# A decoder layer with a state-space mixer: the first pass in another order, and the parameters' copy one step earlier

## What is computed

```python
proj = layernorm(x) @ in_proj_w.T                # 512 -> 8192 gate, 8192 x, 1024 B, 1024 C, 128 step sizes
xBC = silu(causal_conv4(xBC) + conv_b)           # one filter of four taps for each channel
dt = softplus(dt + dt_bias); dA = dt * -exp(A_log)
cum = cumsum(dA)                                 # along the tokens, in chunks
y = ((C @ B.T) * exp(cum_i - cum_j) * mask * dt_j) @ xs + carried state + D * xs
g = y * silu(gate)
x = x + (g * rsqrt(mean(g*g over each of 8 groups) + eps) * norm_w) @ out_w.T
x = x + attention(layernorm(x), ctx, ctx, mask)  # 32 heads of 16, 8 key heads
x = x + low_rank_experts(layernorm(x))           # 4 experts of rank 16, the best 2
```

## Time and profile before

| | us |
|---|---|
| median of 3 runs (2894.97 to 2895.59) | 2895.23 |
| the profiled execution | 2893.02 |
| its span, first to last instruction | 2891.1 |
| TensorE busy | 2826.7 (98%) |
| VectorE busy | 2017.2 (70%) |
| ScalarE busy | 1455.9 (50%) |
| GpSimd busy | 1321.6 (46%) |

### The profile page before, as it was taken

The page is one execution under the profiler, slowest core; times in us unless marked ns, Lnnn a source line. Parts: engine busy times, 40 slices in busy tenths (PEclk is TensorE's granted clock), DMA queues, the critical chain, the costliest instruction groups (busy, mean ns, idle before and its releaser), DMA issues.

```text
span 2891.1 us, 56353 instructions
## 1 busy us (share of the span) xinstructions
PE 2826.7 (98%) x22240; PEld 2284.6 (79%) x22240; DVE 2017.2 (70%) x3156; ACT 1455.9 (50%) x2188; POOL 1321.6 (46%) x832
## 2 busy tenths in 40 slices
PE   6899999999999999999999999999999999999996
PEld 5788878778788888887888888888887888888875
DVE  7677778887667666677666666677666666666657
ACT  5566666565445535445445454544554355454433
POOL 3668767775443433443443443433443343443423
PEclk9999999999999999999999999999999999999997
DMA  6787877878555565555555564555665565665520
GB/s 227 267 305 263 276 258 243 280 264 282 190 193 179 184 195 172 185 190 183 196 196 183 189 201 161 190 189 176 199 199 179 183 193 177 191 196 169 186 92 19
DMA packets 179427, 578.26 MB, mean 200 GB/s; under 512 B 25248, under 2 KB 31904, under 8 KB 171104
## 3 DMA queue, kind: packets, MB, share of 16 engines
q1 hardware_dynamic: 179168, 574.66, 60.2%
HBM read 460.29 MB, written 114.29 MB: 199 GB/s over the span
## 4 chain that ended last, share of the span: by engine, by line
PE 90%; DVE 6%; ACT 2%; issue 1%; DMA 0%; POOL 0%; SPq 0%; DVEq 0%; ACTq 0%; POOLq 0%
PE p_in L464 52%; PE p_out L464 23%; PE p_y L464 9%; PE p_in L552 4%; DVE cv L1311 1%; PE p_y L658 1%; DVE t_y L1360 1%; DVE o_ring L1251 0%; DVE cum L1273 0%; DVE sc L1468 0%; DVE sm L1483 0%; DVE decay L1337 0%; DVE mx L1476 0%; ACT L858 0%; ACT cv L858 0%
## 5 line engine op out<-in xcount | busy, mean ns | idle before, releaser
L464 PE MATMUL p_in<-xnb,w_ring 128*128 128x512 f32 x6864 | 1685.6, 398 | 6.5 <-DVE cv L1311 5.0
L464 PEld LDWEIGHTS p_in<-xnb,w_ring 128*128 128x128 f32 x6864 | 1263.6, 189 | 274.9 <-issue 9.0
L1311 DVE SCALAR_TENSOR_TENSOR cv<-p_in,cpar,cv 128x504 f32<-128x504 f32 x954 | 700.0, 734 | 466.3 <-ACT cv L858 442.6
L1704 POOL TENSOR_TENSOR g_lo<-g_f,g_hi 128x512 fp32r<-128x512 f32 x256 | 341.3, 1335 | 1227.6 <-ACT g_hi L858 1227.6
L464 PE MATMUL p_out<-o_ring,g_hi 128*128 128x512 f32 x2048 | 640.4, 394 | 0.0
L858 ACT ACTIVATE cv<-p_in,cpar 128x512 f32<-128x512 f32 x318 | 246.4, 775 | 653.1 <-PE p_in L464 595.1
L464 PEld LDWEIGHTS p_out<-o_ring,g_hi 128*128 128x128 f32 x2048 | 380.8, 188 | 81.0
L464 PE MATMUL p_out<-o_ring,g_lo 128*128 128x512 f32 x1024 | 400.7, 391 | 0.0
L1348 DVE TENSOR_TENSOR x_tok<-p_in,dts 128x512 f32<-128x512 f32 x256 | 176.6, 690 | 295.0 <-PE p_in L552 293.2
L858 ACT ACTIVATE x_t<-cv 128x512 f32<-128x512 f32 x256 | 160.9, 628 | 305.1 <-DVE t_y L1360 285.7
L1715 POOL TENSOR_TENSOR ss<-ss,g_sq 128x512 f32<-128x512 f32 x190 | 309.8, 1630 | 7.5
(11 more groups left out here) (253 smaller groups left out, 2278.3 us busy)
## 6 DMA issues: line engine op xcount, KB each, us to landing
w_ring<-ws_scr SPq DMA_DIRECT2D x432, 512.0 KB, 3.7
o_ring<-ows_scr SPq DMA_DIRECT2D x192, 512.0 KB, 4.7
ws_scr<-w_ring SPq DMA_DIRECT2D x144, 512.0 KB, 5.7
decay<-cum_scr SPq DMA_DIRECT2D x126, 512.0 KB, 6.6
raw_w<-wt SPq DMA_DIRECT2D x144, 256.0 KB, 4.9
ows_scr<-o_ring SPq DMA_DIRECT2D x64, 512.0 KB, 5.9
raw_o<-owt SPq DMA_DIRECT2D x64, 256.5 KB, 5.2
acb<-x SPq DMA_DIRECT2D x3, 1024.0 KB, 7.9
```

Of the source, the lines that this page charges most:

```text
L464: return nc.tensor.matmul(o, lhsT=l, rhs=r, start=first, stop=last)
L1311: ins = V.scalar_tensor_tensor(acc[:, :, t:SEQ], src[:, :, 0:SEQ - t], cpar[:, 5 * m + 3 - t:5 * m + 4 - t], acc[:, :, t:SEQ], ALU.mult, A ...
L1704: T(g_lo[:, c % 2, :], g_f[:, c % 2, :], g_hi[:, c % 2, :].bitcast(F32), ALU.subtract).then_inc(glo_done, 1)
```

## The change

It edits only the order of the lists, and two waits. Lines of the code that are not named stay.

```diff
-        FIRST_SPLITS = 3
+        FIRST_SPLITS = 5
...
@@ SyncE: body
-                    later_units = () if first(n) and step < 0 else units_of(step)
+                    later_units = units_of(step)
                     if tb == 0 and step == 2:
                         later_units = ()
+                    outs_first = tb == 0 and (step == 3 or first(n) and step == 1)
+                    if outs_first:
+                        refill_outs(step)
                     if tb == 0 and step == 3:
-                        refill_outs(step)
                         later_units = units_of(2) + units_of(3)
...
-                    if tb >= 1 or step != 3:
+                    if not outs_first:
                         refill_outs(step)
             load_next_x(QT)
-            for k in units_of(-1):
-                split_unit(0, k)
             store_cum(0)
@@ TensorE: body, first pass
                     by_token(0)
-                    unit(6, tb, g, n)
                     state_products(n)
                     to_tokens(0, n)
+                    unit(6, tb, g, n)
                     to_tokens(1, n)
@@ ScalarE: body
                     tap0(1, n)
-                    refill(-1)
                     silu_table()
...
                     tap0(3, n)
+                    refill(-1)
                     silu(2, n)
...
-                    if (k == 2 and (...)) or k == 3 or (k == 4 and (is_at(tb, g, 4) or not begun)) \
+                    if (k == 2 and (...)) or k == 3 or (k == 4 and (tb >= 1 and is_at(tb, g, 4) or not begun)) \
...
+                    if k == 7 and tb == 0 and is_at(tb, g, 4):
+                        exp_steps(1)
                     if k == 7 and not final(n):
                         exp(0, n + 1)
...
-                    if k == 3 and is_at(tb, g, 4):
+                    if k == 3 and tb >= 1 and is_at(tb, g, 4):
                         exp_steps(tb + 1)
@@ VectorE
-            softplus(0, (*range(16), 17, 18, 16))
+            softplus(0, (*range(16), 17, 18))
...
-                if tb == 0 and is_at(tb, g, 4) and k in (4, 6, 7):
-                    softplus(1, {4: (0,), 6: (1,), 7: (2,)}[k])
+                if tb == 0 and is_at(tb, g, 4) and k == 7:
+                    softplus(1, (0,))
                 if tb == 0 and is_at(tb, g, 5) and k in (0, 2, 3, 4, 6, 7):
-                    softplus(1, {0: (3,), 2: (4, 5), 3: (6,), 4: (7, 8), 6: (9,), 7: (10, 11, 12)}[k])
-                if tb == 0 and is_at(tb, g, 6) and k in (0, 2, 3, 4, 6):
-                    softplus(1, {0: (13,), 2: (14, 15), 3: (16,), 4: (17,), 6: (18,)}[k])
+                    softplus(1, {0: (1,), 2: (2,), 3: (3,), 4: (4, 5), 6: (6,), 7: (7, 8)}[k])
+                if tb == 0 and is_at(tb, g, 6) and k in (0, 2, 3, 4, 6, 7):
+                    softplus(1, {0: (9,), 2: (10,), 3: (11,), 4: (12, 13), 6: (14, 15), 7: (16, 17, 18)}[k])
...
                 conv(1, n)
+                if not begun:
+                    softplus(0, (16,))
...
+                if not begun:
+                    clamped_half(0)
                 x_tokens(0, n)
...
                 else:
-                    clamped_half(0)
                     x_tokens(1, n)
...
+                    if k == CPG - 1 and not final(n):
+                        parameters((g + 1) % GROUPS if isinstance(g, int) else g + 1)
                     if k > 3:
                         spread(k, tb, g)
                     if k != 3:
                         refill_o(k)
-                    if k == (1 if begun else 3):
+                    if k == 1:
                         clamped(1, n)
...
                     late(k, tb, g)
+                    if k == 2 and not begun:
+                        clamped(1, n)
...
-                if not final(n):
-                    parameters((g + 1) % GROUPS if isinstance(g, int) else g + 1)
@@ GpSimd
                 pool.wait_ge(first_in[half], 32)
-                pool.wait_ge(dtk_done, 2)
+                if half == 0:
+                    pool.wait_ge(dtk_done, 2)
+                else:
+                    pool.wait_ge(clamp_first, 1)
...
-                    if k == (1 if begun else 2) and coming(tb, g) is not None:
+                    if k == 1 and begun and coming(tb, g) is not None:
                         deviation(coming(tb, g))
+                    if k == 1 and tb == 0 and begun:
+                        pool.wait_ge(clamp_done, 2 * n + 2)
                     if begun or k != 2:
                         refill(k - 1)
+                    else:
+                        differences(tb, g, 1, n)
...
+                        if k == 2 and not begun:
+                            deviation(coming(tb, g))
+                            refill(1)
...
-                    if k == 2 and not begun:
-                        refill(1)
-                        differences(tb, g, 1, n)
```

2 lines of the change are left out of this document (1 added, 1 removed).

## The result

| | before | changed |
|---|---|---|
| median (6 runs each, same chip) | 2895.41 us (2894.40 to 2898.67) | 2879.02 us (2877.08 to 2881.84) |
| ratio | | 0.9939, 95% interval 0.9929 to 0.9949 |
| profiled execution, its span | 2893.02, 2891.1 us | 2877.08, 2875.3 us |

The kernel is faster by 0.6%, 16.4 us by these medians. 12.4 were forecast.

What follows compares the result with a forecast made beforehand. TensorE's work, clock and waits were taken to bound the kernel. Gains of 6.5 + 1.0 + 1.7 + 1.7 + 2.2 - 0.7 = 12.4 us gave a median of 2882.8 us, range 2878 to 2889.5.

Steps and rivals of the forecast that it cites:

- part 3: Opening, heads(0) to heads(2): the difference moves into GpSimd's idle time; heads(2) near 72.4 us, or 74.6 if VectorE is held up.
- parts 7 and 8: Passes: earlier parameters' copy, 2.5 less 0.8 lost at pass 7, gains 1.7; GpSimd waiting for the clamp gains 2.2 us.
- Part 1: First softplus: three VectorE operations freed of GpSimd's low halves, 2.8 us earlier, scan ending near 33.2.
- Part 2: Opening up to heads(0): no gain; unit 6 starts near 43.7, takes 5.46 us at low clock, heads(0) at 51.8.
- rival A: VectorE is held up everywhere beside GpSimd, heads(2) gains nothing; 6 us in all, 2889.2 us; chance 0.20.
- Part 4: Opening, to step 4's transposition: with outputs first on SyncE it comes 7.3 or 5.8 us earlier; 6.5 taken.
- Part 5: Clock behind the stop at 89 us: the stop shrinks and 1.0 us (0 to 2) comes back.
- Part 6: Block 1's exponential, moved from step 3 of pass 4 to step 7, shares a table load; gain 1.7 us.
- part 9: Other softplus portions: a reciprocal moved into pass 5 meets a chain without slack; 0.7 us lost (0 to 1.5).
- B: Rival: everything comes back, unit 6 at full clock, VectorE free, pass 7 early; 16.5 us, 2878.7 us; chance 0.12.
- C: Rival: the waits only move to the next late engine; 2 us stay, 2893 us; chance 0.07.
- D: Rival: low clock lasts up to step 4, costing 16 us; the end 4 to 8 us later, 2901; chance 0.04.

Runs made afterwards that it cites:

- e11: The changed kernel with the opening's early weight splits and the place of unit 6 undone; 2878.90 us.
- e10: The changed kernel with the first pass's full clamp behind xnb of step 3 and the deviation directly behind the difference; 2876.12 us, ratio 0.9937.
- e3: The changed kernel with the exponential of block 1 back in step 3 of pass 4; 2882.32 us.
- e14: The changed kernel with block 1's exponential back in step 3 of pass 4 and the old softplus portions; 2879.70 us.
- e4: The changed kernel with the parameters' copy back at the end of the pass; 2888.14 us.
- e5: The changed kernel without GpSimd's wait for the clamp in step 1 of passes 1 to 7; 2885.29 us.
- e6: The kernel before with one edit, the parameters' copy in step 7; 2892.59 us.
- e9: The changed kernel timed again, with no edit undone; 2880.43 us, ratio 0.9949.
- e2: The changed kernel with every edit of the passes undone, only the opening's kept; 2889.69 us, ratio 0.9981.
- e13: The changed kernel with SyncE again serving the output weights behind units 10 and 11 in the first pass; 2882.26 us.

## Why the prediction was right or wrong

The direction and the split into halves were right. The size came out short, 12.4 against 16.4 us, or 13.4 in the second timing. Two steps failed: part 3, which gained nothing up to `heads(2)`, and the sum of parts 7 and 8, with the ceiling of 7.5 us that it was made under. Of the 3.5 us that the two profiled executions differ beyond the forecast, all but 0.2 has a place: the passes make 2.8, the opening -0.4, the stretch behind pass 8 makes 1.8 by chance, and the later first unit -0.8.

- **Part 1, the softplus**: the three operations were as forecast, but the gain was 1.9 us and not 2.8. The scan ended at 34.9, 34.1 without the later start, against 33.2: cum<-d_e ahead of the reciprocal now takes 1.37 beside GpSimd's low halves, 0.43 before, and part 1 did not count it. e11 shows that the gain brings nothing forward here, as part 2 had it.
- **Part 2**: right in its end. `heads(0)` at 52.5, 51.7 without the later start; 51.8 was forecast. In part this is luck: unit 6 started 1.2 us later than forecast (45.73, 44.9 without the later start, against 43.7) and took 4.34 us, 1.1 less than the 5.46.
- **Part 3 failed.** `heads(2)` was forecast between 72.4 and 74.6 and came at 77.1, past the 76 at which I had called myself wrong. The step "the change puts the difference into that idle time" was wrong: the difference waited for its DMA and started at 57.14, and it and g_lo behind it ran beside VectorE. An earlier start helps little: in e11 it followed at once, the pair g_f took 4.87 us, and `heads(2)` came 0.8 us sooner by the unit's clock. The forecast's "held up" priced that pair alone, 3.35 us, and here it was not held up. The half clamp, two low halves and full clamp were, 1.63, 3.49 and 2.29 us, where they take 0.69, 1.48 (twice 0.74) and 1.22 free: 4.0 us, against the 3.7 that rival A gave these three, and about what `heads(2)` is late against the 72.4 for a free VectorE (3.9 without the later start). e10 shows the remedy: with the full clamp behind xnb `heads(2)` comes 5.4 us sooner by the unit's clock, at 70.9 in the times of this part.
- **Part 4**: right in its end. 84.0, 83.2 without the later start, against 81.8 or 83.3, and no wait for raw_o. The loss of part 3 was made good on the way: from 71.90 to there TensorE ran without a pause. The rule of the Trainium skill ("SBUF — State Buffer", section "Who interferes with whom"), an exclusive lock by which this part would be 5.8 and not 7.3, came nearer: the transposition is 6.0 us earlier by the unit's clock (89.14 less 83.97, and the 0.8). That is luck, for the pair to which I applied it was free, and the loss came from other operations, the clamps with one input from SBUF among them.
- **Part 5**: right for this place. The transposition took 0.63 and two units 3.01 and 3.00, against 1.09 and 6.81, 1.3 us for 1.0. But the stop did not shrink, it moved: behind the new one the unit at 72.67 took 4.49 in place of 3.0, 1.5 us that this part did not have.
- Opening in sum: forecast 7.5, measured 7.1 and 6.8.
- **Part 6**: 1.7 forecast, 1.87 by e3.
- **Parts 7 and 8 are the terms that were mis-sized.** For copy and clamp I counted 2.5 + 2.2, and 0.95 more had pass 7 started freely, 5.65 in all. e14, which has copy and clamp but neither exponential nor portions, is 6.9 us shorter in B than before. What failed is the step "So what the first block can give back behind the opening is 7.5 us": it took the list of waits for all there was. The list did what was forecast, 2.2 us are left of it where 1 to 3 were expected, but the passes gave 1.9 us more than it lost, of which about 1.3 were pauses at the starts of passes that no bracket shows in full. And the two were costed as independent, which e4, e5 and e6 refute: alone the copy is worth 0.9, beside the other edits 7.9.
- **Part 7's loss at pass 7 and part 9**: 1.75 and 0.7 forecast, together 2.45; 2.0 to 2.3 measured, all at pass 7, where the wait in brackets is 0.95 and not the 2 expected. Part 9's loss in pass 5 did not come.
- Passes in sum: forecast 4.9 in a range of 3 to 7, measured 7.7 and, in e9, 6.8.
- The remainder of the first timing, some 1.8 us behind pass 8, is chance that no part could hold, and the range ended only 0.7 us below B.

Rival A's price was paid in part, ahead of step 3 only. B came nearest in the first timing, by luck, for none of its reasons held: unit 6 was not at full clock, VectorE was not free, pass 7 did not start early. C and D did not happen; the clock was at 1.00 from 58 to 66 us. D's 0.22 us for each matmul is 0.205 by its own rows, which makes its 16 us 15.

## What to carry to other kernels

Take the ceiling of a gain from distances between rows that both ends of a stretch have, not from the list of waits alone: a row of many matmuls can hide a pause, and a bracket can be smaller than what the wait cost. When two edits touch the same chain of engines, measure them singly and together; here one was worth 0.9 or 7.9 us depending on what was beside it, and two others 1.9 and 0.9 singly but 6.3 together. When an experiment undoes an edit, write down everything that it moves back: two of these moved the low halves of two units as well, and by the rows it was those that moved SyncE's request.

## What the runs showed of the hardware

VectorE and GpSimd beside each other: started 0.10 us ahead of GpSimd's, a 128x512 low half took 0.74 us, started 0.04 ahead 1.88. At 0.06 both were seen, 0.74 in the kernel before (at 483.10) and 1.90 in e2 (at 562.17), so the starts as recorded do not decide it nearer than that. An edit far from it can turn this in every pass; with e6 it did, and its waits for the gate grew by 3.4 us over seven passes.

The twelve matmuls of the step sizes, at 15 us, took 3.0 us in eight of the nineteen profiled executions and 4.7 to 5.3 in eleven, from nearly the same start. TensorE's timeline of the changed kernel

```profile
15.18 3.02 PE L464 MATMUL p_y<-xnb,wd 128*128 128x512 f32 x12 [0.78 <-ACT xnb L858]
```

and of e11:

```profile
14.98 5.21 PE L466 MATMUL p_y<-xnb,wd 128*128 128x512 f32 x12 [0.78 <-ACT xnb L860]
```

The code up to there differs only in splits on another engine, and e13, which does not differ there at all, has 5.15. The granted clock reads 1.00 from 15 to 20 us in all three, so it does not explain this, and the cause stays open. It is 2 us of chance in the time of any single execution of this kernel, and the reason why the distances above are counted from the first unit.
